# A fused attention and mixture-of-experts block on one NeuronCore: two narrow key tiles per score bank, and row maxima of half the key columns from key differences

## What is computed

```python
h = _layernorm(x, axis=-1) * (1 + ca) + sa
Q, K, V = split_heads(h @ W_q.T), split_heads(h @ W_k.T), split_heads(h @ W_v.T)   # 16 heads of 8
Q, K = _rope(Q, pos), _rope(K, pos)
score = einsum('bnqd,bnkd->bnqk', Q, K) / sqrt(8)
score = where(causal, -inf, score)          # causal mask over 1024 x 1024
attn = softmax(score, axis=-1)
out = einsum('bnqk,bnkd->bnqd', attn, V)
x = x + ga * (out.reshape(b, s, 128) @ W_o.T)
h = _layernorm(x, axis=-1) * (1 + cb) + sb
x = x + gb * ffn(h)      # a shared expert and the best 2 of 7 routed experts, width 352
```

## Time and profile before

| | us |
|---|---|
| median of 3 runs | 888.37 |
| the profiled execution | 888.85 |
| its span, first to last instruction | 887.2 |
| projections | 0 to 67 |
| first maxima | 67.5 to 101.7 |
| quad 0 | 101.7 to 129.0 |
| quads 1 to 13 | 129.0 to 465.5 |
| quads 14 and 15 | 465.5 to 519.4 |
| second norm, router, experts | to 887.2 |

### The profile page before, as it was taken

How to read it: one execution, slowest core, us unless ns; L and a number is a source line. 1 busy time by engine, 2 the same in 40 slices (tenths; PEclk the granted TensorE clock), 3 DMA queues, 4 the chain that set the end, 5 groups by cost and what they waited for, 6 DMA issues and landing times. The chain is left out here.

```text
span 887.2 us, 17735 instructions
## 1 busy us (share of the span) xinstructions
PE 730.6 (82%) x5168; PEld 390.4 (44%) x5168; DVE 604.8 (68%) x1906; ACT 518.0 (58%) x1001; POOL 329.8 (37%) x539
## 2 busy tenths in 40 slices
PE   3998899999999999999999876804856769999980
PEld 2551222222222222222223345603646668999870
DVE  5899899999999999999998244602752223333452
ACT  3771387777777777777777685303413345666550
POOL 1348123233222222222221232571054666666562
PEclk9996599999999999999999996966998999999995
DMA  9243200111110011111000790110021222222525
GB/s 238 82 154 120 62 19 22 38 38 38 39 34 23 22 38 38 38 38 33 23 23 2 142 186 14 53 58 27 19 78 54 63 61 67 66 66 64 155 89 145
DMA packets 64759, 56.99 MB, mean 64 GB/s; under 512 B 10798, under 2 KB 52398, under 8 KB 64668
## 3 DMA queue, kind: packets, MB, share of 16 engines
q1 hardware_dynamic: 58924, 44.40, 19.8%
q0 software_dynamic: 4480, 9.64, 3.0%
q10 hardware_dynamic: 1264, 1.84, 0.6%
HBM read 31.90 MB, written 23.55 MB: 62 GB/s over the span
## 5 line engine op out<-in xcount | busy, mean ns | idle before, releaser
L875 ACT ACTIVATE probs<-ps 128x1024 f32<-128x1024 f32 (+3 forms) x384 | 294.4, 812 | 104.5 <-PE ps L1568 103.7
L1108 DVE CUSTOM_DVE_ANT_0 junk<-ps,tri 128x512 f32<-128x512 f32 (+3 forms) x512 | 217.9, 487 | 8.2 <-PE ps L1494 7.2
L1494 PE MATMUL ps<-ka,qa 61*128 61x512 bf16 (+3 forms) x768 | 203.5, 345 | 21.0 <-DVE leftmax L1134 6.3
L1568 PE MATMUL ps<-qa,ka 64*128 64x512 bf16 (+3 forms) x768 | 168.3, 331 | 2.8 <-ACT probs L875 2.3
L1134 DVE TENSOR_REDUCE leftmax<-ps 128x1 f32<-128x512 f32 x256 | 158.8, 684 | 11.8 <-PE ps L1494 10.2
L1546 PE MATMUL ps<-probs,v 128*32 128x512 f32 (+3 forms) x1536 | 165.3, 503 | 0.7 <-POOL probs L705 0.4
L705 POOL TENSOR_SCALAR_AFFINE_SELECT probs<-probs 128x512 f32<-128x512 f32 x128 | 81.2, 634 | 205.3 <-ACT probs L875 205.0
L1494 PEld LDWEIGHTS ps<-ka,qa 61*128 61x128 bf16 x768 | 52.2, 95 | 209.2 <-DVE rowmax L1108 100.2
L771 POOL DMA_INDIRECT routed_results_scratch<-y_s,s_dest x76 | 76.2, 1003 | 62.1 <-issue 56.8
L712 POOL DMA_INDIRECT slot_rows_scratch<-rows,slot x64 | 62.3, 973 | 90.2 <-DVE slot L1284 71.7
L1734 PE MATMUL ps<-wd,hidT 128*128 (+1 forms) x456 | 65.9, 281 | 19.2 <-ACT hidT L1003 19.2
(11 more groups left out here) (184 smaller groups left out, 1041.9 us busy)
## 6 DMA issues: line engine op xcount, KB each, us to landing
slot_rows_scratch<-cst SPq DMA_DIRECT2D x1, 5396.0 KB, 35.0
srow<-slot_rows_scratch SPq DMA_DIRECT2D x76, 71.0 KB
q_parts_scratch<-qk_parts SPq DMA_DIRECT2D x12, 256.0 KB, 2.4
k_parts_scratch<-qk_parts SPq DMA_DIRECT2D x12, 256.0 KB, 2.4
qa<-q_parts_scratch SPq DMA_DIRECT2D x32, 96.0 KB
...
```

What stands on the lines that cost most here:

```text
L875: nc.scalar.activation(probs[s % 4][:, 2 * h:2 * h + 2, 0:CH - q0], ps[:, 2 * h:2 * h + 2, q0:CH], ACT.Exp, scale=SCALE).then_inc(s_exp, 1)
L1108: last = V.tensor_tensor_reduce(out=junk[:, bank - 5, at:at + w], in0=ps[:, bank, at:at + w], in1=tri[:, CH - w:CH], scale=1.0, scalar=LOW ...
L1494: last = MM(ps[:, bank, at:at + w], qa[m][g0:g0 + KS, c0 + q * T:c0 + (q + 1) * T], ka[m][g0:g0 + KS, c0 + k0:c0 + k0 + w], start=True, st ...
L1568: last = MM(ps[:, 2 * pair + g, q0:CH], ka[m][g * HG:(g + 1) * HG, at + kb * T:at + (kb + 1) * T], qa[m][g * HG:(g + 1) * HG, at + c * CH ...
```

## The change

**Steps.** A quad has ten steps instead of twelve. Key tiles 1 and 3 of chunk 0 (384 and 128 wide) share one step and one pair of banks, and key tiles 5 and 7 of chunk 1 as well: tile 3 (or 7) is written to columns 0 to 127 that tile 1 (or 5) leaves free. One exponential covers both. The order of steps becomes, in chunk 0, 0, 2, 1+3, and in chunk 1, 0, 1, 2, 6, 3, 4, 5+7. Eight steps are 512 wide and two (tile 2 of chunk 0, tile 6 of chunk 1) 256. The `probs` buffer goes by the running number of the step.

**Key differences.** For batch row after batch row, `kd` holds keys 0 to 255 minus keys 256 to 511, split into three bfloat16 parts like the keys (GpSimd subtracts, ScalarE copies) and stored behind the 1024 keys: rows of ka are 1280 wide (KW) instead of 1024. With it max(a, b) = b + relu(a - b): for query tiles 6 and 7, TensorE writes the product of queries and key differences into columns 0 to 255 of the score banks of the 256-wide steps (in step 1 for quad n+1's second two heads, in step 6 for quad n+2's first two), ScalarE applies Relu into the buffer `above`, and in the ring the piece "left" holds the products with keys 256 to 511 for both query tiles. VectorE adds `above` and takes the maximum, 256 columns an instruction. Query tiles 4 and 5 stay plain. Before the first step, quad 0 takes all four query tiles this way and quad 1 its first two heads' tiles 6 and 7, with the differences through the ring ("diff").

**Order.** Slots are now equal shares of the cost. The near list has also the left pieces of both pairs of heads. The shift of quad n+1 goes behind one far piece instead of three. The norm entry of the quad before moves from the start of step 3 to that of step 4 (of ten).

```diff
+DW = CH // 2
+KW = S + DW
...
-STEPS = [(c, k, max(0, k - CG * c) * T) for c in range(S // CH) for k in range(CG * (c + 1))]
+def key_tile(c, k, at=None):
+    q0 = max(0, k - CG * c) * T
+    return c, k, q0, q0 if at is None else at
+STEPS = [[key_tile(0, 0)], [key_tile(0, 2)], [key_tile(0, 1), key_tile(0, 3, 0)],
+         [key_tile(1, 0)], [key_tile(1, 1)], [key_tile(1, 2)], [key_tile(1, 6)], [key_tile(1, 3)], [key_tile(1, 4)],
+         [key_tile(1, 5), key_tile(1, 7, 0)]]
 NS = len(STEPS)
+FROM = [min(at for _, _, _, at in tiles) for tiles in STEPS]
+UNTIL = [max(at + CH - q0 for _, _, q0, at in tiles) for tiles in STEPS]
+CHUNK_END = [sum(tiles[0][0] <= c for tiles in STEPS) for c in range(S // CH)]
+MASKED = [sum(k >= CG * c for tiles in STEPS[:s + 1] for c, k, _, _ in tiles) for s in range(NS)]
...
-STEP_COST = 60
 RING = 3
-def head_pieces(j):
-    order = [("masked" if bank[0][3] else "plain", tuple((q, k0, w) for q, k0, w, _ in bank)) for bank in HEAD_BANKS]
-    return [(kind, 2 * j + g, what) for kind, what in order for g in range(2)]
+PAIRED = ((7, 6), (7, 6))
+SPARE_BANKS = [[(s, p) for s in range(NS) if STEPS[s][0][0] == 1 - j and FROM[s] >= DW for p in range(2)] for j in range(HC)]
+DIFF_AT = {at: (2 - j, j, q) for j in range(2) for at, q in zip(SPARE_BANKS[j], PAIRED[j])}
...
+def halves(rows):
+    rows = sorted(rows, reverse=True)
+    return [tuple(sorted(rows[k:k + 2])) for k in range(0, len(rows), 2)]
+def whole_pieces(j, paired):
+    masked = [("masked", 2 * j + g, tuple((q, k0, w) for q, k0, w, _ in bank))
+              for bank in HEAD_BANKS if bank[0][3] for g in range(2)]
+    return masked + [("plain", 2 * j + g, ((q, 0, CH),)) for q in range(CG, TB) if q not in paired for g in range(2)]
+def left_pieces(j, paired):
+    return [("left", 2 * j + g, rows) for rows in halves(paired) for g in range(2)]
+def early_pieces(j, paired):
+    inner, units, out = whole_pieces(j, paired), halves(paired), []
+    for t, rows in enumerate(units):
+        part = inner[len(inner) * t // len(units):len(inner) * (t + 1) // len(units)]
+        out += [("diff", 2 * j + g, rows) for g in range(2)] + part[:2]
+        out += [("left", 2 * j + g, rows) for g in range(2)] + part[2:]
+    return out
...
-    return sum(w + 70 for _, _, w in what)
+    return len(what) * (DW + 75) if kind == "left" else sum(w + 70 for _, _, w in what)
 def quad_pieces(n):
-    near = [("max", n + 1) + x for x in head_pieces(1)] if n + 1 < NQ else []
-    far = [("max", n + 2) + x for x in head_pieces(0)] if n + 2 < NQ else []
-    whole = sum(piece_cost(k, w) for j in range(HC) for k, _, w in head_pieces(j))
-    slots, total = [], 0
-    for s, (_, _, q0) in enumerate(STEPS):
-        for j in range(SLOTS):
-            total += STEP_COST + CH - q0
-            slots.append((total, s * SLOTS + j))
+    near = [(n + 1,) + x for x in left_pieces(0, PAIRED[0]) + whole_pieces(1, PAIRED[1]) + left_pieces(1, PAIRED[1])]
+    far = [(n + 2,) + x for x in whole_pieces(0, PAIRED[0])]
+    whole = sum(piece_cost(k, w) for _, k, _, w in near + far)
+    near, far = near if n + 1 < NQ else [], far if n + 2 < NQ else []
+    slots = [((x + 1) / (NS * SLOTS), x) for x in range(NS * SLOTS)]
     plan, at = [], 0
-    for k, (_, group, kind, h, what) in enumerate(near + far):
-        slot = next((x for end, x in slots if at < end * whole / total), NS * SLOTS - 1)
-        if near and k == len(near) + min(3, len(far)):
+    for k, (group, kind, h, what) in enumerate(near + far):
+        slot = next((x for end, x in slots if at < end * whole), NS * SLOTS - 1)
+        if kind == "left" and h >= 2:
...
+            slot = max(slot, (SPARE_BANKS[1][0][0] + 1) * SLOTS)
+        if near and k == len(near) + min(1, len(far)):
...
-        plan.append((8 * SLOTS, "shift", n + 1, None, None))
+        plan.append((7 * SLOTS, "shift", n + 1, None, None))
...
-        if x == 3 * SLOTS and n:
+        if x == 4 * SLOTS and n:
...
-    out = [(None, kind, 0, h, what) for j in range(HC) for kind, h, what in head_pieces(j)]
+    out = [(None, kind, 0, h, what) for j in range(HC) for kind, h, what in early_pieces(j, range(CG, TB))]
     out.append((None, "shift", 0, None, None))
-    return out + [(None, kind, 1, h, what) for kind, h, what in head_pieces(0)]
+    early = early_pieces(0, PAIRED[0])
+    return out + [(None, kind, 1, h, what) for kind, h, what in early if kind != "left"]
...
+BY_ACT = {kind: [x for x, e in enumerate(RING_PIECES) if e[1] == kind] for kind in ("shift", "diff")}
+BY_DVE = [x for x, e in enumerate(RING_PIECES) if e[1] not in BY_ACT]
+TAKEN = {x: t for which in (BY_DVE, *BY_ACT.values()) for t, x in enumerate(which)}
+LEFT_OF = {(e[2], e[3], q): x for x, e in enumerate(RING_PIECES) if e[1] == "left" for q in e[4]}
+ABOVE = [[(RING_PIECES[x][2], RING_PIECES[x][3], q) for q in RING_PIECES[x][4]] for x in BY_ACT["diff"]]
+ABOVE += [[(n + ahead, 2 * j + g, q) for g in range(2)] for n in range(NQ) for _, (ahead, j, q) in sorted(DIFF_AT.items()) if n + ahead < NQ]
+ABOVE_AT = {key: t for t, keys in enumerate(ABOVE) for key in keys}
...
+        above = sb("above", [T, HQ, TB - CG, DW], at=att)
+        kd = sb("kd", [128, 2, DW], at=att)
...
+                        if w:
+                            sp.wait_ge((s_kd_hi, s_kd_mid, s_kd_low)[p], b + 1)
...
-                        sp.dma_start(dst, qk_parts[:, b % 2, w, p, :]).then_inc(s_spill[b % 2], 16)
+                        sp.dma_start(dst, qk_parts[:, b % 2, w, p, 0:KW if w else S]).then_inc(s_spill[b % 2], 16)
...
+                if n % 2 == 0:
+                    pool.wait_ge(s_sum, n * 2 + 2)
+                    k_rows = rot[:, 0, 1, 0, :]
+                    nc.gpsimd.tensor_tensor(kd[:, 0, :], k_rows[:, 0:DW], k_rows[:, DW:CH], ALU.subtract).then_inc(s_kd, 1)
...
+                    pool.wait_ge(s_kd_hi, b + 1)
+                    nc.gpsimd.tensor_tensor(kd[:, 1, :], kd[:, 0, :], qk_parts[:, b % 2, 1, 0, S:KW], ALU.subtract).then_inc(s_kd_rest, 1)
+                else:
+                    pool.wait_ge(s_kd_mid, b + 1)
+                    nc.gpsimd.tensor_tensor(qk_parts[:, b % 2, 1, 2, S:KW], kd[:, 1, :], qk_parts[:, b % 2, 1, 1, S:KW],
+                                            ALU.subtract).then_inc(s_kd_low, 1)
...
+                    for c, k, q0, at in tiles:
+                        if k < CG * c:
+                            continue
+                        pool.wait_ge(s_exp, n * (2 * NS) + 2 * (s + 1))
+                        pool.sem_inc(s_seen_pool, 1)
+                        p = probs[(n * NS + s) % 4][:, :, at - FROM[s]:at - FROM[s] + T]
+                        nc.gpsimd.affine_select(out=p, in_=p, compare_op=ALU.is_ge, fill=0.0, base=0,
+                                                pattern=[[0, HQ], [1, T]], channel_multiplier=-1).then_inc(s_mask, 1)
...
+                if u == 1:
+                    act.wait_ge(s_kd_rest, b + 1)
+                    nc.scalar.activation(qk_parts[:, b % 2, 1, 1, S:KW], kd[:, 1, :], ACT.Copy).then_inc(s_kd_mid, 1)
...
+                if u == 0:
+                    act.wait_ge(s_kd, b + 1)
+                    nc.scalar.activation(qk_parts[:, b % 2, 1, 0, S:KW], kd[:, 0, :], ACT.Copy).then_inc(s_kd_hi, 1)
...
+            def room_above(keys):
+                if keys[0][0]:
+                    ring_taken(act, max(LEFT_OF[n - 1, h, q] for n, h, q in keys))
+            def keep_above(x):
+                _, _, n, h, rows = RING_PIECES[x]
+                room_above(ABOVE[TAKEN[x]])
+                ring_written(act, x)
+                nc.scalar.activation(above[:, h, rows[0] - CG:rows[-1] - CG + 1, :],
+                                     ps[:, ring_bank(x), 0:len(rows) * DW].rearrange("p (q w) -> p q w", w=DW), ACT.Relu).then_inc(s_above, 1)
+            def keep_beside(n, s, p):
+                ahead, j, q = DIFF_AT[s, p]
+                if n + ahead < NQ:
+                    room_above(ABOVE[ABOVE_AT[n + ahead, 2 * j, q]])
+                    nc.scalar.activation(above[:, 2 * j:2 * j + 2, q - CG, :], ps[:, 2 * p:2 * p + 2, 0:DW], ACT.Relu).then_inc(s_above, 1)
...
-                        nc.scalar.activation(probs[s % 4][:, 2 * h:2 * h + 2, 0:CH - q0], ps[:, 2 * h:2 * h + 2, q0:CH],
+                        if (s, h) in DIFF_AT:
+                            keep_beside(n, s, h)
+                        nc.scalar.activation(probs[(n * NS + s) % 4][:, 2 * h:2 * h + 2, 0:UNTIL[s] - FROM[s]], ps[:, 2 * h:2 * h + 2, FROM[s]:UNTIL[s]],
                                              ACT.Exp, scale=SCALE).then_inc(s_exp, 1)
...
-                    if s == 5:
+                    if s == CHUNK_END[0] + 1:
...
+            for x in RING_AT["first"]:
+                if RING_PIECES[x][1] == "diff":
+                    keep_above(x)
+                elif RING_PIECES[x][1] == "shift":
+                    shift_out(0)
...
+                    elif kind == "left":
```

(26 more changed lines are left out.)

86 lines of the change are left out of this document (38 added, 48 removed).

## The result

The changed kernel takes 859.36 us (median of four runs, 859.07 to 859.5) against 888.42 in the same rounds: a ratio of 0.9671, with a 95% interval of 0.9651 to 0.969. The forecast was 856. The profiled execution took 859.44 us, its span is 857.7.

The account below looks back on a forecast made before the run. VectorE was taken to bound the steady quads: 13 x 1.8 = 23.4 us saved there, 2 in quad 0, 4 at the start and 3 at the end make 32.4, from 888.85 to a median of 856; range 842 to 876.

Parts of the forecast that it names:

- The bound before: Steady quads: VectorE, busy 24.70 of 25.88 us, sets the pace; ScalarE's waits mostly follow from it.
- Part 1: VectorE's maxima in a steady quad: eight reductions become fused add-and-max at 0.35 us; work falls from 24.7 to 22.6 us.
- Part 2: ScalarE in a steady quad: pairing saves 0.4 us, four Relus add 2.4; work goes from 19.64 to 21.7 us.
- D: Rival, steady quads: ScalarE's waits come from TensorE's order and stay, so Relu adds time, 913 us; chance 0.06.
- E: Rival, ScalarE in attention: Relu outside the exponential's table forces table loads, 10.3 us a quad, about 970; chance 0.02.
- Part 3: TensorE and its queue: columns stay the same, eight more matmuls hide, spare steps' banks free one Relu (0.59 us) later.
- A: The forecast itself: VectorE bounds the steady quads, 23.6 to 24.6 us each, 849 to 863 in all; chance 0.56.
- B: Rival: short steps' hand-overs caused VectorE's gaps; steady quads of 22.8 to 23.3 us, 840 to 848 in all; chance 0.12.
- C: Rival: TensorE and ScalarE give half the gain back; steady quads of 24.7 to 25.8 us, 864 to 888; chance 0.24.
- Part 4: Moved waits in steady quads: nothing new waits for the key loads; the row shift keeps some 3 us to spare.
- Part 5, the start: Before the first exponential: ScalarE's copies add 1.6 us, GpSimd's subtractions hide in waiting, shorter maxima save; net -4 us.
- Part 5, quads 14 and 15: Last two quads, where VectorE is not the bound: two steps fewer save hand-overs, 1.5 us each, -3 together.

Follow-up runs that it names:

- the differences alone: The change's key differences kept, but with twelve steps a quad in the order of before: 891.02 us, ratio 1.000 to the kernel before.
- masked pieces leading: Changed kernel with only the order of the first maxima edited: masked pieces first, difference pieces spread among them; 794.77 us, ratio 0.9563 to the kernel before.

## Why the prediction was right, and where it was not

**The bound before.** "A steady quad is therefore worth what VectorE saves in it" was half of it. VectorE's work did bound, but the same 2.1 us saved without pairing brought 0.23. The last half of that sentence, "until TensorE or ScalarE comes up from below", had its distance wrong: at twelve steps they were already there. The row on which I leaned, four exponentials with no wait between them, stands in wide steps, and says nothing of the narrow ones. So the saving on VectorE could show only because the change also shortened that loop by two steps, and the sum gave their hand-overs no term in the steady quad.

**Part 1** held. The new form starts every 0.34 to 0.35 us, and VectorE's work is 22.45 us a quad (forecast 22.6). The timeline of DVE, changed kernel:

```profile
74.26 0.42 DVE L1235 CUSTOM_DVE_ANT_0 junk<-ps,above 128x256 f32<-128x256 f32 x1
74.61 0.08 DVE L1235 DVE_READ_ACCUMULATOR2_ANT leftmax<- 128x1 f32 x1
74.61 0.42 DVE L1235 CUSTOM_DVE_ANT_0 junk<-ps,above 128x256 f32<-128x256 f32 x1
```

**Part 2** held. The Relu takes 0.60 us (forecast 0.59), ScalarE's work is 21.12 (21.7), with one table load in the attention. D and E fell with it.

**Part 3** had the largest mis-sized term. I priced the hand-overs of two steps only as waiting that might vanish, and added idle time to VectorE (1.5 us) because the others came nearer. They came nearer in work but the loop had become shorter: VectorE's idle time is 23.43 - 22.45 = 1.0 us. With 0.5 less idle time and 0.15 less work than forecast the quad is 23.43 instead of 24.1. The quad lies between A's 23.6 and B's 23.3: A's mechanism with B's cause for the gaps. C, the largest rival with a chance of 0.24, describes the differences alone (25.65), not the change.

**Part 4** held: no wait for the key loads or the shift shows in a steady quad of the changed kernel.

**Part 5, the start**, failed in two terms. "GpSimd's 12 subtractions ... lie in its 46.1 us of waiting" was true of GpSimd and missed VectorE: the subtractions delay it, and the first maxima start 3.45 us later. Of the forecast's 1.6 for ScalarE's copies little or nothing came: with the copies and without the subtractions they start at 67.53, as before the change. And the forecast took the stage behind as 16 x 0.26 us shorter than its 22.9 us (67.54 to 90.44); it is 23.15. The stage before, in the changed kernel and with masked pieces leading (behind the length stand the busy times of PE, PEld and VectorE):

```profile
67.54:90.44 22.90, 18.39 (x43) 3.48 (x42) 22.87 (x80) 1.56 (x4) 18.74 (x14) 0.62 0.26 99
```
```profile
70.99:94.14 23.15, 16.83 (x58) 3.56 (x58) 19.11 (x97) 5.67 (x11) 19.17 (x15) 0.58 0.22 83
```
```profile
70.93:92.17 21.24, 17.18 (x59) 4.40 (x58) 19.45 (x97) 5.99 (x11) 19.38 (x15) 0.60 0.22 86
```

VectorE's work fell by 3.8 us, near the forecast's 4.2, but its idle time went from 0.0 to 4.0. The forecast had put that term at nothing. Difference pieces that hold ring banks are 1.9 to 2.2 us of it, by the order that leads with masked pieces; the rest is open. Start and stage together are 94.14 instead of 87.9 for the last combination. From there to the first exponential it is 10.5 us, as forecast (10.7), so +2.0 in place of -4.

**Part 5, quads 14 and 15** held (-3.4, forecast -3). **After the attention**, "isn't touched" is true of the code of that part and not of the time: +5.7 us, 1.2 of them by the change.

The sum: -8.1 in the quads 1 to 13, -0.3 in quad 0 and -0.4 in quads 14 and 15 against the forecast, +6.0 at the start and +5.7 at the end, together +2.9: 859.3 for 856.4.
